# Projecting the queries of two rows at once in the rows without GELUs of a gated cross-attention kernel

## The reference

```
x = x + tanh(g_xattn) * xattn(layernorm(x), ctx, ctx)      16 heads of 16
x = x + tanh(g_ffn) * ffn(layernorm(x))                    BitLinear, 256 -> 1024 -> 256
xattn: Q = LN(x) Wq + bq;  K = ctx Wk + bk;  V = ctx Wv + bv;  qk = Q K^T per head
  feats = (mean of scores, mean of the row maxima, mean variance of softmax(scores))
  log_t = clip(w3 gelu(w2 gelu(w1 feats + b1) + b2) + b3);  t = exp(log_t) per head
  out = softmax(qk / (2 t)) V;  nan_to_num;  out Wo + bo
```

## Time and profile before

| | |
|---|---|
| median of 3 runs | 797.61 us (792.31 to 798.23) |
| profiled execution | 792.8 us, of which the span is 791.0 |
| PE busy | 702.7 us, 89% |
| DVE busy | 708.0 us, 90% |
| ACT busy | 683.9 us, 86% |
| POOL busy | 487.9 us, 62% |

### The profile page before, as it was taken

One profiled execution on the slowest core, in us unless ns is written; L12 is line 12 of the kernel. 1 busy time (PEld: TensorE's weight loads), 2 busy tenths in 40 slices (PEclk: granted clock), 3 DMA queues, 4 the chain that ended last, 5 costly groups with the idle time before them and its releaser, 6 DMA issues.

```text
span 791.0 us, 20866 instructions
## 1 busy us (share of the span) xinstructions
PE 702.7 (89%) x7118; PEld 474.6 (60%) x7127; DVE 708.0 (90%) x1452; ACT 683.9 (86%) x1454; POOL 487.9 (62%) x956
## 2 busy tenths in 40 slices
PE   6567899999999999999999999999999888877896
PEld 4334566666666666667676766676765555533453
DVE  5779899989899999999999999899999776798995
ACT  1578899898999999999999999999999888768883
POOL 4747657667777667676766666767664043245663
PEclk9666899999999999999999999999999899999998
DMA  9997747464668575767455666656664122246688
GB/s 206 204 261 166 197 127 149 109 126 128 154 120 149 124 144 124 145 122 158 123 138 134 134 137 133 128 136 130 124 118 85 39 68 86 71 103 164 160 179 181
DMA packets 148887, 108.50 MB, mean 137 GB/s; under 512 B 56991, under 2 KB 145183, under 8 KB 148767
## 3 DMA queue, kind: packets, MB, share of 16 engines
q1 hardware_dynamic: 143630, 101.98, 58.3%
q10 hardware_dynamic: 5152, 5.19, 2.7%
HBM read 49.54 MB, written 12.85 MB: 79 GB/s over the span
## 4 chain that ended last, share of the span: by engine, by line
PE 36%; ACT 35%; DVE 16%; issue 9%; DMA 2%; ACTq 1%; POOL 1%; SPq 0%; DVEq 0%; POOLq 0%
ACT ex L1197 13%; ACT pt L1187 12%; PE p_o L1348 7%; PE p_m L1426 6%; PE p_s L1328 5%; PE p_m L1407 5%; PE p_t L1369 4%; DVE kst L1032 3%; DVE hmax L1035 3%; PE p_m L1415 3%; ACT L1223 3%; ACT L1187 2%; DVE stats L907 2%; PE p_m L1399 2%; DVE nm L926 2%
## 5 line engine op out<-in xcount | busy, mean ns | idle before, releaser
L1197 ACT ACTIVATE ex<-p_s,nm 112x375 f32<-112x375 f32 x512 | 275.8, 618 | 12.3 <-DVE nm L926 11.0
L1187 ACT ACTIVATE pt<-p_t,ct 128x336 f32<-128x336 f32 x488 | 245.8, 577 | 26.7 <-PE p_t L1369 24.5
L907 DVE BATCH_NORM_STATS2 stats<-ex 112x6 f32<-112x375 f32 x512 | 252.5, 535 | 1.4 <-ACT ex L1197 1.3
L926 DVE TENSOR_REDUCE nm<-p_s 112x2 f32<-112x750 f32 x256 | 236.0, 922 | 1.2 <-PE p_s L1328 1.0
L1328 PE MATMUL p_s<-kst,qst 96*112 96x375 bf16 x512 | 154.8, 348 | 13.5 <-ACT ex L1197 7.3
L1369 PE MATMUL p_t<-qst,kst 99*128 99x112 bf16 x1464 | 115.1, 213 | 4.9 <-ACT pt L1187 4.0
L1369 PEld LDWEIGHTS p_t<-qst,kst 99*128 99x128 bf16 x1464 | 91.1, 98 | 44.0 <-issue 19.7
L1407 PE MATMUL p_m<-wv_sb,ctxt 128*128 128x256 f32 (+1 forms) x384 | 106.7, 401 | 4.7 <-DVE va L859 2.9
L1348 PE MATMUL p_o<-pt,va 128*32 128x112 f32 (+1 forms) x3072 | 101.7, 265 | 1.4 <-ACT pt L1187 0.8
L1426 PE MATMUL p_m<-ctxt,wk_sb 128*128 128x375 f32 x240 | 94.6, 518 | 1.7 <-DVE qf L875 1.1
L1328 PEld LDWEIGHTS p_s<-kst,qst 96*112 96x112 bf16 x512 | 67.0, 139 | 45.7 <-ACT ex L1197 34.6
(11 more groups left out here) (187 smaller groups left out, 1164.3 us busy)
## 6 DMA issues: line engine op xcount, KB each, us to landing
kst<-kp SPq DMA_DIRECT2D x378, 93.8 KB, 3.5
ctxt<-ctxt_dram SPq DMA_DIRECT2D x32, 375.0 KB, 4.2
qbounce<-qp SPq DMA_DIRECT2D x32, 168.0 KB, 2.5
qst<-qbounce SPq DMA_DIRECT2D x32, 168.0 KB, 3.6
qst<-qbounce SPq DMA_DIRECT2D x32, 112.0 KB, 3.4
xm<-x_dram SPq DMA_DIRECT2D x32, 112.0 KB, 2.4
x_dram<-x SPq DMA_DIRECT2D x32, 112.0 KB, 1.9
xt<-x_dram SPq DMA_DIRECT2D x28, 128.0 KB, 3.2
```

The lines of the kernel that those rows point to most:

```text
L907: last = nc.vector.bn_stats(stats[:, nb % RING, 2 * pb + i], ex[0:SQ, 2 * (t % 2) + i, :])
L926: nc.vector.tensor_reduce(nm[:, n % RING, 2 * p:2 * p + 2], p_s[t % 2][0:SQ, :, 0:SK], axis=AX.X, op=ALU.max, negate=True).then_inc(s_max, 1)
L1187: nc.scalar.activation(pt[:, (2 * r + i) % 8], st_home(r, i)[:, 0:KC * SQ].rearrange("k (c q) -> k c q", c=KC), ACT.Exp, scale=ct[:, nr % ...
L1197: nc.scalar.activation(ex[0:SQ, 2 * ((t - 1) % 2) + i, :], p_s[(t - 1) % 2][0:SQ, i, 0:SK], ACT.Exp, bias=nm[:, ne % RING, h:h + 1]).then_ ...
```

## The change

Q of two rows is projected in slot 1 of each odd row (`projected`): rows n + 2 and n + 3, as one set of four matmuls with 224 columns. Even rows have no Q. Row 10, the first whose norm comes from another group, is kept alone, so rows 9, 10, 31 and the first three (0, 1, 2) are projected singly and 26 rows in 13 pairs. The bias is added for both rows by one instruction of 448 elements in slot 2, the sum moves to slot 3 (one instruction, or two where the ring `sumq` wraps), and `split_q` works on both rows. `event` counts projections rather than rows. x is transposed in slot 7 of the even row and slot 0 of the odd row behind it, for which GpSimd normalizes it in slots 5 and 7 of the even row. The bounce of Q to DRAM moves from slot 4 to slot 5, and the load of `xa` in even rows from slot 5 to slot 1. `qf` and `xnt` get two halves; `onn`, `ltc` and `st2` give up their memory, and the guard works in place.

```diff
         def active(piece, n):
-            return 0 <= n + OF[piece] < B
+            return 0 <= n + OF[piece] < B and (piece != "Q" or n <= 0 or n % 2 == 1 or n + Q_AHEAD == LN_REST)
+        def projected(n):
+            first = n + Q_AHEAD
+            pair = n > 0 and first + 1 < B and LN_REST not in (first, first + 1)
+            return range(first, first + (2 if pair else 1)) if active("Q", n) else range(0)
+        def event(f):
+            return f if f < SINGLES else SINGLES + (f - SINGLES) // 2 + (f >= LN_REST)
-        def queries_at(n):
-            return 0 if roomy_row(n - 1) else 1
         def turned(t):
             n, p = divmod(t, SLOTS)
-            x = n + 1 + Q_AHEAD if p == 7 and pair_of(n) else n + Q_AHEAD if p == 0 and not pair_of(n - 1) else B
+            x = n + Q_AHEAD if p == 0 and (n <= 0 or n + Q_AHEAD == LN_REST) else n + 3 if n >= 0 and p == (7 if n % 2 == 0 else 0) and n + 3 != LN_REST else B
+        def normed(t):
+            x = 2 if t == X2_AT else n + 3 if p == 5 else n + 4 if p == 7 and n + 4 != LN_REST else B
...
 # sync
-                if p == 4 and 0 < f < B:
+                if p == 4 and 0 < f < B and n <= 0:
                     bounce_q(f)
-                if p == 5 and HOMED <= n + 4 < B:
+                if p == (1 if n % 2 == 0 else 5) and HOMED <= n + 4 < B:
...
+                if p == 5 and 0 < f < B and n > 0:
+                    bounce_q(f)
 # gpsimd
-                if p == 3 and 0 < n + Q_AHEAD < B:
-                    split_q(n + Q_AHEAD)
+                if p == 3 and n + Q_AHEAD > 0 and projected(n):
+                    split_q(projected(n))
 # vector
-                if p == queries_at(n) + 1 and 0 <= n + Q_AHEAD < B:
+                if p == 2 and rows:
...
+                    nc.vector.tensor_tensor(qf[:, of].rearrange("p j c q -> p c j q"),
+                                            p_m[:, 0:C * len(rows) * SQ].rearrange("p (c j q) -> p c j q", c=C, q=SQ),
+                                            bq[:, :].unsqueeze(2).unsqueeze(3).to_broadcast([P, C, len(rows), SQ]), ALU.add).then_inc(s_qc, 1)
+                if p == (3 if n > 0 else 2) and rows:
...
+                    if len(rows) == 2 and first % SRING < SRING - 1:
+                        nc.vector.tensor_reduce(sumq[:, first % SRING:first % SRING + 2, :], qf[:, :], axis=AX.X, op=ALU.add).then_inc(s_qs, 1)
+                    else:
+                        for i, f in enumerate(rows):
+                            last = nc.vector.tensor_reduce(sumq[:, f % SRING, :], qf[:, j + i], axis=AX.X, op=ALU.add)
+                        last.then_inc(s_qs, 1)
 # tensor
-                if p == queries_at(n) and active("Q", n):
+                if p == 1 and rows:
                     take("Q", n)
...
-                            last = mm(p_m[:, c * SQ:(c + 1) * SQ], wq[:, k, c * P:(c + 1) * P], xnt[:, k, :], start=(k == 0), stop=(k == C - 1))
+                            last = mm(p_m[:, c * wide:(c + 1) * wide], wq[:, k, c * P:(c + 1) * P], xnt[:, of, k, :], start=(k == 0), stop=(k == C - 1))
```

More of the change, by code:

```diff
@@ L323, in emptied @@
             return {
-                "Q": (s_qc, count(1, b, 1)),
+                "Q": (s_qc, count(1, event(b), 1)),
                 "V0": (s_vc, count(3, b, 1)), "V1": (s_vc, count(3, b, 2)), "V2": (s_vc, count(3, b, 3)),
@@ L578, in split_k, with split_q @@
                 nc.gpsimd.tensor_tensor(lo, kf[:, c], mid, ALU.subtract).then_inc(s_kp2, 1)
[L580 to L587, removed]
+            def split_q(rows):
+                first, e = rows[0], event(rows[0])
+                pool.wait_ge(s_qc, count(1, e, 1))
+                if first >= 2:
+                    pool.wait_ge(s_qd, count(16, first - 3 + len(rows), 16))
+                of = slice((first + 1) % 2, (first + 1) % 2 + len(rows))
+                lo, mid, hi = (qp[:, of, i] for i in range(PARTS))
+                done = count(3, e)
+                nc.gpsimd.tensor_scalar(hi, qf[:, of], 1.0, 0.0, ALU.mult, ALU.add).then_inc(s_qx, 1)
                 pool.wait_ge(s_qx, done + 1)
-                pool.wait_ge(s_qs, count(1, b, 1))
-                nc.gpsimd.tensor_tensor(qf[:, :, :], qf[:, :, :], hi, ALU.subtract).then_inc(s_qx, 1)
+                pool.wait_ge(s_qs, count(1, e, 1))
+                nc.gpsimd.tensor_tensor(qf[:, of], qf[:, of], hi, ALU.subtract).then_inc(s_qx, 1)
                 pool.wait_ge(s_qx, done + 2)
-                nc.gpsimd.tensor_scalar(mid, qf[:, :, :], 1.0, 0.0, ALU.mult, ALU.add).then_inc(s_qx, 1)
+                nc.gpsimd.tensor_scalar(mid, qf[:, of], 1.0, 0.0, ALU.mult, ALU.add).then_inc(s_qx, 1)
                 pool.wait_ge(s_qx, done + 3)
-                nc.gpsimd.tensor_tensor(lo, qf[:, :, :], mid, ALU.subtract).then_inc(s_qp2, 1)
+                nc.gpsimd.tensor_tensor(lo, qf[:, of], mid, ALU.subtract).then_inc(s_qp2, 1)
             odd, even = float(SK // 2), float(SK - SK // 2)
@@ L670, in slot @@
                     nc.gpsimd.tensor_tensor(fd[:, :], fd[:, :], fc[:, :], ALU.mult).then_inc(s_feat, 1)
-                if (p == 5 and n >= 0 or t == X2_AT) and 1 < n + 3 < B:
-                    x = n + 3
+                x = normed(t)
+                if x is not None:
                     pool.wait_ge(s_ln, LN_ALL if x >= LN_REST else 4 * ln_group(x) + 4)
@@ L792, in split_first_q @@
             def split_first_q():
-                lo, mid, hi = (qp[:, 0, i] for i in range(PARTS))
-                chain(nc.vector.tensor_copy(hi, qf[:, :, :]), s_qx, 1)
+                lo, mid, hi = (qp[:, 1, i] for i in range(PARTS))
+                chain(nc.vector.tensor_copy(hi, qf[:, 1]), s_qx, 1)
                 dve.wait_ge(s_qs, 1)
-                chain(nc.vector.tensor_tensor(qf[:, :, :], qf[:, :, :], hi, ALU.subtract), s_qx, 2)
-                chain(nc.vector.tensor_copy(mid, qf[:, :, :]), s_qx, 3)
-                nc.vector.tensor_tensor(lo, qf[:, :, :], mid, ALU.subtract).then_inc(s_qp2, 1)
+                chain(nc.vector.tensor_tensor(qf[:, 1], qf[:, 1], hi, ALU.subtract), s_qx, 2)
+                chain(nc.vector.tensor_copy(mid, qf[:, 1]), s_qx, 3)
+                nc.vector.tensor_tensor(lo, qf[:, 1], mid, ALU.subtract).then_inc(s_qp2, 1)
             def split_first_k():
@@ L920, in slot @@
                     dve.wait_ge(s_xt, count(1, x, 1))
[L921 to L923 removed]
+                    if x > 1:
+                        dve.wait_ge(s_qmm, count(1, event(x - 2), 1))
+                    nc.vector.tensor_copy(xnt[:, (x + 1) % 2], ride[t % 2]).then_inc(s_xtc, 1)
                 if 0 <= t < SLOTS * B:
@@ L1390, in slot @@
                     mm(t_h2, w2t[:, :], hid1[:, :], start=True, stop=True).then_inc(s_h2, 1)
-                if p == queries_at(n) and active("Q", n):
+                rows = projected(n)
+                if p == 1 and rows:
                     take("Q", n)
@@ L1395, in slot @@
                         pe.wait_ge(s_pre, WQ)
-                    pe.wait_ge(s_xtc, count(1, n + Q_AHEAD, 1))
+                    pe.wait_ge(s_xtc, count(1, rows[-1], 1))
+                    of, wide = slice((rows[0] + 1) % 2, (rows[0] + 1) % 2 + len(rows)), len(rows) * SQ
                     for c in range(C):
                         for k in range(C):
-                            last = mm(p_m[:, c * SQ:(c + 1) * SQ], wq[:, k, c * P:(c + 1) * P], xnt[:, k, :], start=(k == 0), stop=(k == C - 1))
+                            last = mm(p_m[:, c * wide:(c + 1) * wide], wq[:, k, c * P:(c + 1) * P], xnt[:, of, k, :], start=(k == 0), stop=(k == C - 1))
                     last.then_inc(s_qmm, 1)
```

45 lines of the change are left out of this document (24 added, 21 removed).

## The result

| | before | after |
|---|---|---|
| median, same chip | 797.92 us (792.31 to 798.84, 4 runs) | 811.31 us (809.52 to 813.55, 4 runs) |
| ratio | | 1.0184, 95% interval 1.0131 to 1.0238 |
| profiled execution | 792.8 us, span 791.0 | 809.52 us, span 807.6 |

The change makes the kernel 13.4 us slower by the medians; 9.2 were forecast. (The ratio is not the quotient of the two medians, which is 1.0168.) The period from one GELU table load to the next, two rows, is 38.94 us instead of 38.04. The first fence is the busy time by stretch of the changed kernel: rows 19 and 20, the odd row, the even row (columns as in the earlier trace rows).

A forecast was written before the change was run, and what follows sets the result against it. PE, DVE and ACT are within 2 us of the 38.0 us period, so waits per slot decide. Eleven pairs at 0.70 us (+7.7) plus rows 7 and 29 (+1.5) give +9.2: median 797.6 to 806.8 us, range 798 to 814.

The forecast's parts named there:

- The sign and the mechanism: Pair in slot 1 of the odd row costs 1.75 us, even row returns 1.05; slower by over 1%, chance 0.53.
- The projection's length: Slot 1 of the odd row: eight records of 224 columns take 1.55 us, bounds 0.99 and 1.98.
- The odd row: Odd row about 1.75 us longer, with transposed scores, addition, K0 and K1 all later behind the pair's projection.
- The split of that sum: Odd row's 1.75 us: 1.2 on ACT, then 0.2 for K0 and 0.35 for K1.
- The even row: Q gone from slot 1 returns 1.05 us: 0.79 at slot 2, then K0's wait 0.17 and slot 6 0.1.
- The start: The earlier load of `xa` moves within the slack and costs nothing.
- the early pairs: Pairs of rows 1 and 3, before the second pass: 0, give or take 1.5 us.
- Rows 7 and 8: Row 7 projects one row in slot 1 instead of 0: wait 0.64 us, with the addition's delay about 0.75.
- A: Wide projection costs no more than one row: +0.2 us a pair, +3.7 in all, time 801.3; chance 0.15.
- B: Pair's Q starts by 392.7 in slot 1, odd row costs nothing: -12.6 us, time 785; chance 0.11.
- C: GpSimd's norm in slot 7 becomes late: 1.2 us a pair on top, +22 us; chance 0.02.
- Rows 7 and 29: One row projected in slot 1 instead of 0, no even row relieved: about 0.75 us each, +1.5.

The follow-up runs named there:

- e2: e1 with each row's queries projected alone again in slots 0 and 1, only the moves left: 793.96 us against 797.22 before, ratio 0.9961.
- e7: e1 with the pair projected in slot 0 from row 11 on, x transposed and normalized earlier: 796.59 us against 793.54 before, ratio 1.0038.
- e3: e1 with the transposed scores ahead of the pair's projection in slot 1: 811.23 us against 797.22 before, ratio 1.0177.
- e4: e1 with the bias addition behind the statistics of slot 2 on VectorE: 804.41 us against 797.22 before, ratio 1.0099.
- e1: Changed kernel with row 4 of x loaded at the start of the program: 808.50 us against 797.22 before, ratio 1.0143.
- e9: Kernel before up to row 10, then pairs in slot 0 of odd rows, addition behind slot 1's statistics: 790.81 us against 795.93 before, ratio 0.9964.
- e10: e2 run again on the chip of e9 in more rounds: 793.50 us against 795.93 before, ratio 1.0000.
- e6: e1 projecting only the first row's queries and using them for both, results wrong: 799.23 us in one run against a median of 793.54 before.

## Why the prediction was right, and where it was off

- **The sign and the mechanism.** A move from slot 0 to slot 1 of the odd row that costs more than the even row gives back: shown by e2 (all but the pair, 38.04), the change (38.94) and e7 (the same pair in slot 0, 37.62).
- **The projection's length**: 1.55 forecast, 1.62 measured, on the line between 112 and 375 columns (1.64). By the rule of the Trainium skill, page "TensorE: Matmul & The Clock Gate", section "Back-to-back issue gap", for one isolated warm matmul it would have been 0.77 us, counted once for each of the eight records as the prediction did, and half of that for the four matmuls that they are. These f32 records follow neither.
- **The odd row**: forecast 1.75 longer, measured 1.72 (18.17 less 16.45), with each step in its place: addition at 395.73 (forecast 395.66), K0 396.41 (396.4), K1 401.12 (401.1), ACT's wait 1.11 (1.2).
- **The split of that sum** was misread. The prediction gave 1.2 of it to ACT's wait, and 0.2 and 0.35 to K0 and K1. e3 took the wait away and gained nothing; e4 took most of DVE's idle time away and gained 0.19. The delays run side by side, not one behind the other.
- **The even row**: 1.05 forecast to come back, 0.82 measured (16.11 less 15.29). The 0.79 at slot 2 came exactly. Of the further 0.25, K0's wait gave 0.09 instead of 0.17 (1.85 us from the exponentials of slot 2 to K0 on ACT, instead of 1.94), and the wait in slot 6 nothing. So a pair costs 0.90 instead of 0.70: eleven of them 9.9 us instead of 7.7.
- **The start** is the step that failed: "the earlier `xa` ... within that slack" was read from the rows in the middle. In row 0 the load has no slack, and the first GELU load came 6.4 us late (e1: 5.4 of them from the load). By the second, 3.95 us were left, of which e1 lays 2.2 to the load. The forecast had 0 for the early pairs.
- **Rows 7 and 8**: 0.75 forecast, 2.34 measured. The prediction's "from row 6 on, these periods are all 38.0 us" overlooks that the one from row 6 to row 8 lasts 39.57 (and the last two, to rows 30 and 32, 36.79 and 36.08). This period in the kernel before, the changed kernel and e9:

```profile
155.51:195.08 39.57, 37.16 (x413) 25.92 (x412) 35.94 (x72) 37.45 (x84) 28.35 (x57) 1.00 0.58 127
160.07:201.98 41.91, 39.00 (x413) 27.22 (x412) 36.23 (x72) 37.73 (x85) 28.42 (x57) 0.96 0.54 120
157.62:198.09 40.47, 38.16 (x413) 26.84 (x412) 36.10 (x72) 38.01 (x85) 28.37 (x57) 0.96 0.57 124
```

  e9 has the same program here as the kernel before, and e2 (40.50) and e10 (40.48) project in the same slots as it. All three are at 0.96 and take 0.9 us more than the kernel before at 1.00. So about 0.9 of the 2.34 goes with the clock, and about 1.4 is left for the projection of row 9 in slot 1 and the rest of the change, twice the forecast. What makes it so much was not tried.
- **The rivals**: A was measured by e6 at +0.22 a pair, as worked out. B (faster) needed the projection to start 1.2 us earlier, and e7 shows that this was indeed the deciding place; but a pair there gained 0.42 and not 1.05 (B was also added up for 12 pairs, and the sum for 11). C did not occur in the middle rows, though its like did at the start, as a late load.

The medians differ by 13.4 us and the two profiled spans by 16.6; both kernels have stretches at the lower clock at different places, and the profiled execution before was the shortest of its runs. That the forecast's 9.2 lies 4 us under the measurement comes in the main from the pairs (2.2 us) and from the start (some 2). Rows 7 and 29 were forecast at 1.5 together; row 29 with the even row behind it took 0.80, and row 7 with its even row about 1.4 at equal clock.

## What to carry to other kernels

Where three engines are each within some per cent of the period, merging two operations into one wide one is worth what its place leaves: the gap into which the single one fitted was in a slot with room, and the merged one stood in a slot with none. Ask for each slot what stands ahead of the operation, what shares its buffer after it, and what stands behind its reader in that engine's queue. And look at the first rows by themselves: in the middle the load of `xa` is issued 11.0 us ahead of its norm (387.77 to 398.78) and lands in time, and at the start it takes 13.1 us and everything waits for it.

## What was not expected of the hardware

- The small load of x (112 KB) issued at 35.68 us was not there for POOL until 48.99, 13.3 us later, while the weights were being loaded (DMA share 1.08 in the stretch from 44 to 50 us). That the weights' loads held it up is likely but was not tried.
- Stretches at a lower granted clock of PE stand at different places in different kernels. From 166 to 172 us it is 0.81 on the mean in the changed kernel, and 1.00 in the one before, from 155.5 to 195 us. From 612 to 630 us it is 0.81 in the kernel before, and 1.00 in e2; the last period, with the same count of matmul records (364), lasts 36.08 us in the one and 33.17 in the other. So two profiled spans can differ by some us at places that the change doesn't touch, and the periods of the middle rows, all at 1.00, compare kernels better than the spans do.
